# A fused decoder layer on one core: group 0's deviations first on GpSimd, its key copies over three queues

## The reference, cut to what matters

```python
def layer(x, ctx, W):                         # x: 64 x 64 x 256, ctx: 64 x 64 x 64, float32
    x = x + self_attention(layernorm(x))      # 16 query heads of 16, 4 key/value heads, causal
    x = x + cross_attention(layernorm(x), ctx)    # keys and values are ctx itself
    x = x + moe(layernorm(x))                 # 64 experts, 6 chosen, capacity 96, and a shared expert
    return x

def self_attention(x):                        # batch b, head h, key group g = h // 4
    q, k, v = x @ Wq + bq, x @ Wk + bk, x @ Wv + bv
    s = q @ k.T / 4                           # 64 x 64 for each b and h, masked above the diagonal
    return softmax(s) @ v

def layernorm(x):
    return (x - mean(x)) / sqrt(var(x) + 1e-5)
```

## Time and profile before

| what | us |
|---|---|
| median of three runs | 716.64 (714.97 to 718.74) |
| the profiled execution, its own time | 718.88 |
| its span in the trace | 717.0 |
| TensorE busy, share of the span | 639.0, 89% |
| first score matmuls (mask) begin, from the span's start | 36.62 |

### The profile page before, as it was taken

How to read it: one execution, slowest core, us unless ns; L and a number is a source line. 1 busy time by engine, 2 the same in 40 slices (tenths; PEclk the granted TensorE clock), 3 DMA queues, 4 the chain that set the end, 5 groups by cost and what they waited for, 6 DMA issues and landing times. The chain is left out here.

```text
span 717.0 us, 16771 instructions
## 1 busy us (share of the span) xinstructions
PE 639.0 (89%) x6161; PEld 450.4 (63%) x6161; DVE 471.2 (66%) x1278; ACT 332.8 (46%) x634; POOL 341.0 (48%) x374
## 2 busy tenths in 40 slices
PE   1599999999888889988998989899999999999991
PEld 0256666666667666666775445467787778667761
DVE  3157676757878798989896579925455455445463
ACT  2367777776766776776664442222222222222000
POOL 6012321121354443445412256487777777777473
PEclk9899999999999999999999999999999999999996
DMA  8222333343444321332131159239999999844597
GB/s 247 38 45 46 85 83 83 89 101 83 72 109 109 79 66 35 86 75 53 32 99 38 45 155 252 85 94 223 255 250 269 249 249 268 222 76 67 123 358 264
DMA packets 144705, 94.27 MB, mean 131 GB/s; under 512 B 62192, under 2 KB 142320, under 8 KB 144624
## 3 DMA queue, kind: packets, MB, share of 16 engines
q1 hardware_dynamic: 129008, 74.58, 39.7%
q0 software_dynamic: 10240, 14.16, 10.6%
q10 hardware_dynamic: 5376, 4.46, 1.9%
HBM read 60.26 MB, written 24.50 MB: 118 GB/s over the span
## 5 line engine op out<-in xcount | busy, mean ns | idle before, releaser
L1443 POOL DMA_INDIRECT sum_d<-tk,targets x64 | 91.9, 1435 | 29.9 <-issue 14.4
L790 DVE TENSOR_REDUCE mx<-Sc 128x16 f32<-128x1024 f32 x64 | 78.2, 1222 | 36.5 <-PE Sc L434 36.2
L1263 PE MATMUL Sc<-xT,wgu_sb 128*128 128x96 f32 (+1 forms) x768 | 92.8, 271 | 0.0
L658 ACT COPY ET<-ring 128x512 f32<-128x512 f32 x128 | 68.9, 589 | 41.1 <-PE ring L446 38.4
L1263 PEld LDWEIGHTS Sc<-xT,wgu_sb 128*128 128x128 f32 (+1 forms) x768 | 87.2, 187 | 0.4 <-issue 0.4
L462 PEld LDWEIGHTS O<-vbd,ET 128*64 128x64 f32 x2048 | 66.6, 138 | 29.2 <-issue 17.0
L794 DVE TENSOR_TENSOR E<-Sc,mx 128x1024 f32<-128x1024 f32 x64 | 78.4, 1225 | 6.9 <-DVE mx L790 0.5
L446 PE MATMUL ring<-ident,E 128*128 128x128 f32 x512 | 69.5, 279 | 11.9 <-ACT E L697 11.9
L1436 POOL DMA_INDIRECT rows<-rows_d,tokens x64 | 64.2, 1003 | 29.1 <-issue 13.1
L462 PE MATMUL O<-vbd,ET 128*64 128x34 f32 x2048 | 73.6, 225 | 3.2 <-ACT ET L658 2.7
L434 PE MATMUL Sc<-kbd,qT 64*64 64x256 f32 x1024 | 71.9, 384 | 5.0 <-DMA kbd<-kT 5.0
(11 more groups left out here) (208 smaller groups left out, 1195.1 us busy)
## 6 DMA issues: line engine op xcount, KB each, us to landing
wgu_sb<-in_wgu_dram SPq DMA_DIRECT2D x128, 176.0 KB, 3.6
sum_d<-zeros SPq DMA_DIRECT2D x16, 524.0 KB, 5.8
kbd<-kT SPq DMA_DIRECT2D x248, 32.0 KB, 2.2
wda_sb<-in_wd_dram SPq DMA_DIRECT2D x32, 160.0 KB
wgu_sb<-sum_d SPq DMA_DIRECT2D x10, 512.0 KB, 9.5
X<-in_x_dram SPq DMA_DIRECT2D x8, 512.0 KB, 6.5
rows_d<-xhT SPq DMA_DIRECT2D x8, 512.0 KB, 2.9
out_dram<-X ACTq DMA_DIRECT2D x8, 512.0 KB, 6.6
```

What stands on the lines that cost most here:

```text
L658: nc.scalar.copy(ET[:, m % 2, 4 * v:4 * v + 4].rearrange("p j q -> p (j q)"), bank(name)[:]).then_inc(s_act, 1)
L790: nc.vector.reduce_max(mx[:, m % 2, :], sc, AX.X).then_inc(s_mx, 1)
L1263: last = nc.tensor.matmul(GP[e % 2][0:m, CAP * u:CAP * (u + 1)], wgu_cols[j][:, c, m0:m0 + m], xT[:, e % 2, c, :], start=c == 0, stop=c == 1)
L1443: pool.indirect_dma_start(w["sums"][e % 2], bass.IndirectOffsetOnAxis(ap=targets[:, e:e + 1], axis=0), outs[:, e % OB, :], None, compute_o ...
```

## The change

GpSimd does `deviation(0)` first, then clears `kbd[0]` (taken over from VectorE) and `vbd`, adds the ones columns, does `deviation(1)`, waits for `kT`, issues five of group 0's key copies with a semaphore of their own, and clears `kbd[1]` after that. ScalarE issues three of the eight copies instead of all. Both, and SP, now wait for the clearing of `kbd[0]`. SP waits for the later clearing of `kbd[1]` before group 1's key copies. The two iotas of `desc` go from the prologue to `pack_matrix`.

```diff
--- before.py
+++ after.py
@@ -15,6 +15,8 @@
 H, G, D = 16, 4, 16
 NT = B * S // 128
 GT = 4
+FIRST_ACT = 3
+BY_POOL = 16 * (H // 2 - FIRST_ACT)
 NG = NT // GT
 GB = 2 * GT
 TOK = 128 * GT
@@ -232,6 +234,7 @@
     s_dve = sem("ring_dve")
     s_k = sem("keys_saved")
     s_kbd = sem("keys_blocked")
+    s_kbf = sem("first_keys_blocked")
     s_clr = sem("cleared")
     s_vb = sem("values_cross")
     s_sc = sem("scores")
@@ -275,6 +278,12 @@
     ring = Ring(ring_uses())
     KDMA = 16 * H
 
+    def first_keys(eng, h0, h1, signal):
+        for h in range(h0, h1):
+            src = 16 * (2 + h // HQ)
+            eng.dma_start(kbd[0][D * h:D * (h + 1), 1, :, h % HQ, :],
+                          kT[src:src + D, :].rearrange("p (b k) -> p b k", k=S)).then_inc(signal, 16)
+
     def bank(name):
         return banks[ring.bank(name)]
 
@@ -295,6 +304,8 @@
                     sp.wait_ge(s_k, g + 1)
                 else:
                     sp.wait_ge(*saved(("K", g)))
+                if g == 0:
+                    sp.wait_ge(s_clr, 1)
                 if g >= 2:
                     sp.wait_ge(s_sc, 4 * (g - 1))
                 for c in range(1 if g == 0 else 2):
@@ -338,7 +349,7 @@
                 sp.dma_start(X[:, g * GT:(g + 1) * GT, :], x_rows[:, g * GT:(g + 1) * GT, :]).then_inc(s_x, 16)
             for g in range(2 * NG):
                 if g == 1:
-                    sp.wait_ge(s_clr, 1)
+                    sp.wait_ge(s_clr, 5)
                 if routed(g - 3):
                     store_rows(g - 3)
                 if routed(g - 5):
@@ -418,7 +429,9 @@
                 g, t = m // GT, m % GT
                 cross = is_cross(g)
                 if t == 0:
-                    pe.wait_ge(s_kbd, KDMA * (g + 1))
+                    pe.wait_ge(s_kbd, KDMA * (g + 1) - BY_POOL)
+                    if g == 0:
+                        pe.wait_ge(s_kbf, BY_POOL)
                     pe.wait_ge(*saved(("XT1" if cross else "Q1", g)))
                 if m >= 2:
                     pe.wait_ge(s_sub, m - 1)
@@ -511,7 +524,7 @@
             def weights_t(g):
                 out = empty_bank(("WP", g))
                 if g == NG:
-                    pe.wait_ge(s_pk, 1 + BT)
+                    pe.wait_ge(s_pk, 3 + BT)
                 pe.wait_ge(s_te, 5 * (g - NG + 1))
                 for t in range(GT):
                     last = nc.tensor.matmul(out[NE:128, 128 // BT * t:128 // BT * (t + 1)],
@@ -607,7 +620,9 @@
                 name = ("K", g)
                 act.wait_ge(s_fill, ring.filled(name))
                 if g >= 1:
-                    act.wait_ge(s_kbd, KDMA * g)
+                    act.wait_ge(s_kbd, KDMA * g - BY_POOL)
+                if g == 1:
+                    act.wait_ge(s_kbf, BY_POOL)
                 src = bank(name)
                 if is_cross(g):
                     for t in (0, 1):
@@ -618,7 +633,9 @@
                     nc.scalar.activation(kT[:], src[0:64, :], ACT.Identity,
                                          bias=w["bkv_sb"][0:64, :]).then_inc(s_k, 1)
                     if g == 0:
-                        first_keys()
+                        act.wait_ge(s_k, 1)
+                        act.wait_ge(s_clr, 1)
+                        first_keys(nc.scalar, 0, FIRST_ACT, s_kbd)
                     src = src[64:128, :].rearrange("p (b k) -> p b k", k=S)
                     nc.scalar.activation(vT[64:128], src.unsqueeze(2).to_broadcast([64, GB, 2, S]),
                                          ACT.Identity, bias=w["bkv_sb"][64:128, :]).then_inc(s_act, 1)
@@ -695,13 +712,6 @@
             def exp(m):
                 act.wait_ge(s_sub, m + 1)
                 nc.scalar.activation(E_[:, m % 2, :], E_[:, m % 2, :], ACT.Exp).then_inc(s_exp, 1)
-
-            def first_keys():
-                act.wait_ge(s_k, 1)
-                for h in range(HH):
-                    src = 16 * (2 + h // HQ)
-                    act.dma_start(kbd[0][D * h:D * (h + 1), 1, :, h % HQ, :],
-                                  kT[src:src + D, :].rearrange("p (b k) -> p b k", k=S)).then_inc(s_kbd, 16)
 
             def shared_save(k):
                 n, half = MC[k // 2][1], k % 2
@@ -994,17 +1004,30 @@
                                             w["ctx2"][:, i % 2].rearrange("p b (g d) -> p b g d", d=D),
                                             mem["halfmask"][:, h:h + 1], None, ALU.mult).then_inc(s_vb, 1)
 
-            nc.gpsimd.memset(kbd[1][:], 0.0).then_inc(s_clr, 1)
-            pool.wait_ge(s_clr, 1)
+            deviation(0)
+            nc.gpsimd.memset(kbd[0][:], 0.0).then_inc(s_clr, 1)
             nc.gpsimd.memset(vbd[:], 0.0).then_inc(s_clr, 1)
             pool.wait_ge(s_clr, 2)
             for h in range(2):
                 nc.gpsimd.tensor_scalar(vbd[:, :, :, :, h, D], vbd[:, :, :, :, h, D], mem["halfmask"][:, h:h + 1], None,
                                         ALU.add).then_inc(s_clr, 1)
+            deviation(1)
+            pool.wait_ge(s_k, 1)
+            first_keys(nc.gpsimd, FIRST_ACT, HH, s_kbf)
+            nc.gpsimd.memset(kbd[1][:], 0.0).then_inc(s_clr, 1)
             def pack_matrix():
+                for h in range(2):
+                    if h == 0:
+                        pool.wait_ge(s_res, 7)
+                    else:
+                        pool.wait_ge(s_pk, 1)
+                    nc.gpsimd.iota(desc[NE * h:NE * (h + 1), :], pattern=[[-BT * UNIT, NB]],
+                                   base=(NT * 128 - BT * NB * h) * UNIT, channel_multiplier=0,
+                                   allow_small_or_imprecise_dtypes=True).then_inc(s_pk, 1)
+                pool.wait_ge(s_pk, 2)
                 nc.gpsimd.memset(pack[:], 0.0).then_inc(s_pk, 1)
                 for i in range(BT):
-                    pool.wait_ge(s_pk, i + 1)
+                    pool.wait_ge(s_pk, i + 3)
                     nc.gpsimd.affine_select(out=pack[:], in_=pack[:], compare_op=ALU.not_equal,
                                             fill=float(2 ** (BT - 1 - i)), base=-i, pattern=[[-BT, 128 // BT]],
                                             channel_multiplier=1).then_inc(s_pk, 1)
@@ -1012,7 +1035,7 @@
             for m in range(FIRST, LAST):
                 if m == 8:
                     pack_matrix()
-                if m % 4 == 3 and is_self((m + 9) // 4):
+                if m % 4 == 3 and 2 <= (m + 9) // 4 < NG:
                     deviation((m + 9) // 4)
                 if m % 4 == 2 and is_cross((m + 6) // 4):
                     deviation((m + 6) // 4)
@@ -1778,18 +1801,12 @@
                                             channel_multiplier=1).then_inc(s_const, 1)
                 pool.wait_ge(s_const, 3)
                 nc.gpsimd.memset(mem["half_pow"][:], -0.5).then_inc(s_const, 1)
-                for h in range(2):
-                    pool.wait_ge(s_const, 4 + h)
-                    nc.gpsimd.iota(mem["desc"][NE * h:NE * (h + 1), :], pattern=[[-BT * UNIT, NB]],
-                                   base=(NT * 128 - BT * NB * h) * UNIT, channel_multiplier=0,
-                                   allow_small_or_imprecise_dtypes=True).then_inc(s_const, 1)
 
             @block.vector
             def _(dve):
                 for h in range(2):
                     nc.vector.memset(mem["halfmask"][64 * h:64 * (h + 1), h:h + 1], 1.0)
                     nc.vector.memset(mem["halfmask"][64 * h:64 * (h + 1), 1 - h:2 - h], 0.0)
-                nc.vector.memset(mem["kbd"][0][:], 0.0)
                 nc.vector.memset(zeros[:], 0.0)
                 dve.wait_ge(s_const, 1)
                 nc.vector.tensor_copy(mem["ident_bf"][:], mem["ident"][:]).then_inc(s_vconst, 1)
```

## The result

Four runs before and four after: 717.69 us (714.97 to 720.79) against 710.50 us (707.97 to 710.81), medians. The ratio is 0.9879, 95% interval 0.9848 to 0.9911, so the change makes the kernel 1.2% faster, 7.2 us. The forecast was 711.4, range 708.2 to 716.0. The profiled execution went from 718.88 to 710.81 us, its span from 717.0 to 709.0.

The account below looks back on a forecast made before the run. TensorE, busy 639.0 of 717.0 us, bounds the kernel, so edits pay only where it stands still. In the head, GpSimd's copies landing at 31.3 move scores(0) from 36.62 to 31.4, -5.2 us: 716.64 to 711.4, range 708.2 to 716.0.

Parts of the forecast that it names:

- rival C: Group 0's key copies on GpSimd are cheap, 0.9 us apart or less; scores(0) at 28.7, gain 7.9, 708.7 us; chance 0.08.
- Part 1: Prologue: without VectorE's clearing and GpSimd's two iotas the block ends at 4.92 us, gain 1.2, moving all later starts.
- Part 2: Head, group 0: with deviation(0) first, normalization starts at 9.36 us instead of 14.97, and kT is there at 17.3.
- Part 3: GpSimd's fills behind deviation(0): through at 16.1 us, kbd[0] 4.5 us ahead of kT, cost nothing.
- Part 4: Head, group 1: ScalarE waits for deviations held by x; normalization at 22.3 us instead of 30.23, TensorE ready at 28.7.
- Part 5: GpSimd's five copies of group 0's keys: start at 22.2 us, 1.53 apart, the last landing at 31.3.
- C's sign: In the profile after, TensorE released by ScalarE before the mask matmuls would show cheap GpSimd copies; chance 0.08.
- Part 6: Behind GpSimd's copies: kbd[1] cleared from 29.9 to 33.4 us, second kT at 35.2, 1.8 us to spare.
- Part 7: pack_matrix takes 1.18 us plus two gaps longer, covered by 2.17 us idle before the next residual; uncovered, at most 1.8.
- Rival A: GpSimd's first DMA is slow, 4.3 us extra; last copy lands at 35.6, time 714.2 to 715.7 us; chance 0.22.
- Rival B: GpSimd writes every copy slowly, deciding at 2.85 us spacing; at 5.52 apart 13.4 us slower, 730; chance 0.08.
- Rival D: The head's gain doesn't arrive, given back in the first steps of the loop; chance 0.04.

Follow-up runs that it names:

- split semaphore: Group 1's rows of x got a semaphore of their own, against the changed kernel; median 708.23 us, ratio 0.9869 to the kernel before.

## Why the prediction was right

The time came within 0.9 us of the forecast, by a path that the forecast gave a chance of 0.08 only (rival C). Some of the closeness is luck. The forecast took 5.2 us off a median of 716.64; with the fourth run that median is 717.69, and the change took off 7.2. The ratio forecast, 711.4 to 716.64, is 0.9927, above the measured interval of 0.9848 to 0.9911.

*Part 1, the prologue.* Forecast: released at 4.92, gain 1.2. Measured: 5.05, gain 1.07. The loads of x, landed at 18.08 instead of 19.10, gave 1.02.

*Part 2, deviation(0).* Forecast 9.36, measured 9.51. `kT` is saved by 17.50; forecast 17.3.

*Part 3, the fills.* GpSimd is through at 15.90 (forecast 16.1), `kbd[0]` at 12.87. Hidden, as said.

*Part 4, x is what is late next.* Group 1's deviations end at 22.36, normalization starts at 22.39; forecast 22.2 and 22.3. The split semaphore shows the reason. TensorE was then to be ready at 28.7 by the 6.39 us of the earlier trace rows; it took 6.90, since the stretch at 1.2 GHz reached into the transposes (1.06 and 0.93 us instead of 0.78 and 0.71 before).

*Part 5, GpSimd's copies: the term that was mis-sized.* Forecast 1.53 us apart, landed at 31.3, and so what scores(0) waits for. Measured 0.59 apart, landed at 26.9, 2.4 us to spare: TensorE is released neither by a DMA, as was forecast, nor by ScalarE, as C's sign had it, but comes to scores(0) from its own matmuls. The nearest rows were gathers whose 96 rows are looked up in a tile; scaling them by the number of pieces was wrong on both counts, as the direct copy with more pieces costs less than two thirds of one (0.54 against 0.92). Even the lower bound of the spacing, 1.23, was twice the truth. So the mechanism was that of rival C: parts 1 to 4 decide alone. Its scores(0) at 28.7, plus 0.1 for the later normalization and 0.5 for the clock, is the 29.3 measured. The forecast's time was right although its path was not, because C lay only 2.7 us from it.

*Part 6.* `kbd[1]` is clear at 25.28 + 3.54 = 28.82, the second `kT` is saved at 33.20: 4.4 us to spare; forecast 1.8.

*Part 7, pack_matrix.* GpSimd after the change:

```profile
77.14 1.18 POOL L1024 IOTA desc<- 64x512 f32 x2
...
81.66 0.73 POOL L987 TENSOR_TENSOR X<-X,att 128x256 f32<-128x256 f32 x1 [1.04 <-DVE att L820]
```

The idle time before the second residual shrank from 2.17 to 1.04 and hides the iotas.

*Rival A* is refuted twice: GpSimd's first direct copy took 0.81 us, and the first gather is slow for another reason. The Trainium skill's rule of some 6 us for a first call (GPSIMD Engine Reference, Instruction dispatch) speaks of freshly loaded code. No run here shows such a price for a DMA: the first direct copy took 0.81 us and a first gather as little as 1.09. *Rival B* never came near: 0.59 against the 2.85 from which it would decide. *Rival D* is refuted up to the end of the self-attention (7.34 of 7.33); behind it single executions are up to about two microseconds shorter or longer.

## What to carry to other kernels

Ask of a stage's start which wait would be last once the named one is gone, and of a semaphore that counts several transfers whether its first reader needs them all: here one such wait cost 1.6 us directly and 0.9 to 2.3 more through the clock. In the head, where TensorE stands between short bursts, a gain was partly paid in its clock: shifts of 1.4, 2.7 and 0.9 us at a normalization were worth 1.2, 1.8 and 0.5 at the matmuls. A direct copy of 32 KB from GpSimd's queue cost it 0.59 us, like one from the others, but SP's issues beside it were slower, so look at all queues when copies are moved between them. And when a forecast comes out right, compare its path with the trace as well as its time.

## What was not expected of the hardware

A direct copy took GpSimd 0.54 us (the first 0.81) against 0.92 for a gather of 96 rows and 0.60 to 0.62, the shortest and the median, for the same copy on SP's and ScalarE's queues in the changed kernel. With copies on three queues at once single issues of SP took up to 1.00 us, and landings up to 3.9 us; with two queues, in the kernel before, up to 3.4. Beside VectorE's two-input instructions a gather took 2.25 to 5.2 us instead of 0.92, though one slipped through in 1.09, and a tiny GpSimd instruction 1.07 instead of 0.24 us; five direct copies took no longer (2.95 us).
